# Attention and feed-forward kernel: the last two value bursts of a group go one slot forward, the maxima one slot back

## What is computed

```python
q = (seq2 + b_self) @ Wq + bq                     # 16 heads of 32
k = concat([seq1 + b_prev, seq2 + b_self]) @ Wk + bk
v = concat([seq1, seq2]) @ Wv + bv
score_prev = where(mask, q @ k[:l1].T * SCALE, -inf)   # 512 x 512 per head
score_self = (q * k[l1:]).sum(-1) * SCALE              # a row's own key
weights = softmax(concat([score_prev, score_self]))
attn = weights[..., :-1] @ v[:l1] + weights[..., -1:] * v[l1:]
x = x + attn @ Wo + bo
x = x + concat([gelu(x @ W1 + b1) @ W2 + b2, gelu(...) @ We[indices] + be])
```

## Time and profile before

| | |
|---|---|
| time, median of 3 runs | 1796.44 us (1793.42 to 1796.46) |
| profiled execution, its own time | 1807.21 us |
| its span | 1805.1 us |
| granted TensorE clock, mean | 0.976 |
| TensorE (PE) busy | 1719.9 us, 95% |
| VectorE (DVE) busy | 942.4 us, 52% |
| ScalarE (ACT) busy | 709.5 us, 39% |
| GpSimd (POOL) busy | 663.4 us, 37% |

### The profile page before, as it was taken

The page is one execution under the profiler, slowest core; times in us unless marked ns, Lnnn a source line. Parts: engine busy times, 40 slices in busy tenths (PEclk is TensorE's granted clock), DMA queues, the critical chain, the costliest instruction groups (busy, mean ns, idle before and its releaser), DMA issues.

```text
span 1805.1 us, 27962 instructions
## 1 busy us (share of the span) xinstructions
PE 1719.9 (95%) x8256; PEld 1262.1 (70%) x8256; DVE 942.4 (52%) x1430; ACT 709.5 (39%) x1259; POOL 663.4 (37%) x521
## 2 busy tenths in 40 slices
PE   6998999999999999999987899999999999999996
PEld 5765656666666666666652688888888888888885
DVE  4577576775866768757587643232232323232321
ACT  3253454444544445445344443323232323233222
POOL 3165577584874847748564301000010101010101
PEclk8999999999999999999996999999999999999998
DMA  6452444443534435244344342223131413232212
GB/s 143 76 114 51 91 103 107 86 97 73 120 90 91 96 85 119 69 103 87 80 110 121 109 122 50 68 48 86 46 87 41 87 52 75 61 66 72 47 30 53
DMA packets 370269, 149.45 MB, mean 83 GB/s; under 512 B 289226, under 2 KB 329162, under 8 KB 370194
## 3 DMA queue, kind: packets, MB, share of 16 engines
q1 hardware_dynamic: 364966, 146.28, 35.7%
q10 hardware_dynamic: 5228, 2.35, 0.5%
HBM read 70.41 MB, written 27.28 MB: 54 GB/s over the span
## 4 chain that ended last, share of the span: by engine, by line
PE 78%; issue 6%; DVE 5%; DMA 4%; SPq 3%; POOL 2%; ACT 1%; ACTq 0%; DVEq 0%; POOLq 0%
PE ps_proj L1258 14%; PE ps_max L1289 6%; PE ps_av L1210 6%; PE ps_av L1212 6%; PE ps_av L1211 6%; PE ps_av L1329 6%; PE ps_score L1316 5%; PE ps_proj L1210 3%; PE ps_proj L1211 3%; PE ps_proj L1212 3%; DMA stacks<-parts 3%; PE ps_score L1210 3%; PE ps_max L1212 3%; PE ps_score L1212 3%; PE ps_max L1210 3%
## 5 line engine op out<-in xcount | busy, mean ns | idle before, releaser
L729 ACT ACTIVATE p_f<-ps_score 128x512 f32<-128x512 f32 x512 | 303.8, 599 | 459.2 <-PE ps_score L1316 414.8
L941 DVE TENSOR_REDUCE m_col<-ps_max 128x1 f32<-128x512 f32 x512 | 328.7, 683 | 201.2 <-PE ps_max L1289 199.9
L604 POOL TENSOR_TENSOR p_sum<-p_sum,p_f 128x512 f32<-128x512 f32 x256 | 335.4, 1342 | 3.3 <-ACT p_f L729 3.3
L644 POOL TENSOR_TENSOR z_f<-z_f,a_raw 128x512 f32<-128x512 f32 x32 | 40.8, 1287 | 750.5 <-ACT z_f L842 730.0
L1135 DVE TENSOR_TENSOR h_lo<-h_f,h_hi 128x512 fp32r<-128x512 f32 x128 | 88.0, 687 | 412.2 <-ACT h_hi L833 412.1
L601 POOL TENSOR_TENSOR p_sum<-p_f 128x512 f32<-128x512 f32 x128 | 161.6, 1293 | 210.7 <-PE ps_av L1338 205.4
L1289 PE MATMUL ps_max<-stacks 97*128 97x512 f32 x512 | 189.3, 437 | 38.1 <-DVE m_col L941 19.4
L1258 PE MATMUL ps_proj<-in_hi,w_hi 128*128 128x512 f32 x512 | 207.8, 406 | 11.2 <-POOL in_lo L609 7.9
L1316 PE MATMUL ps_score<-stacks 99*128 99x512 f32 x512 | 209.0, 419 | 5.6 <-ACT p_f L729 5.4
L1210 PE MATMUL ps_av<-y_hi,w_hi 128*128 128x512 f32 x512 | 199.9, 390 | 6.6 <-ACT h_hi L833 3.8
L1258 PE MATMUL ps_proj<-in_lo,w_hi 128*128 128x512 f32 x512 | 205.6, 402 | 0.0
(11 more groups left out here) (122 smaller groups left out, 2729.1 us busy)
## 6 DMA issues: line engine op xcount, KB each, us to landing
stacks<-parts SPq DMA_DIRECT2D x384, 128.0 KB
raw<-in_x_dram SPq DMA_DIRECT2D x128, 64.0 KB, 2.3
raw<-in_fside_BxSxS_dram SPq DMA_DIRECT2D x128, 64.0 KB, 2.2
den<-own_scratch SPq DMA_DIRECT2D x128, 64.0 KB, 2.8
attn_scratch<-num SPq DMA_DIRECT2D x32, 256.0 KB, 3.0
x_raw<-in_x_dram SPq DMA_DIRECT2D x128, 64.0 KB, 2.2
we_raw<-in_L_cond_We_dram SPq DMA_DIRECT2D x32, 256.0 KB, 2.8
resid_scratch<-a_raw SPq DMA_DIRECT2D x32, 256.0 KB, 2.0
```

The lines of the kernel that those rows point to most:

```text
L604: pool.tensor_tensor(p_sum[:, j], p_sum[:, j], now, ALU.add).then_inc(sum_made, 1)
L729: act.activation(p_f[:, i % FLIGHT], ps_score[i % 2][:, :], ACT.Exp, scale=SCALE).then_inc(p_made, 1)
L941: dve.tensor_reduce(m_col[:, n % C, n // C:n // C + 1], ps_max[n % 2][:, :], AX.X, ALU.max).then_inc(max_made, 1)
```

## The change

`tiles_of_max` gives slot 0 no tile, and slots 1 to 8 two each; the bursts of `t` 2 and 3 of the group before follow the score (and the third, if there is one) of slot 0. The order of operations inside a slot is as before: score, maxima, values, thirds, bursts.

```diff
@@ -244,7 +244,7 @@
         def tiles_of_max(i):
 
-            ends = (2, 4, 6, 8, 10, 12, 14, TILES)
+            ends = (0, 2, 4, 6, 8, 10, 12, 14, TILES)
             return range(ends[i - 1] if i else 0, ends[i]) if i < len(ends) else range(0)
@@ -1392,7 +1392,7 @@
                         for n in thirds_of(g, i) if more else ():
                             project(*nxt2, order[n // 3], n % 3)
-                        if i == 1 and not (first and g == 0):
+                        if i == 0 and not (first and g == 0):
                             for t in (2, 3):
                                 value_burst(*after(b, g, -1), t)
```

## The result

The changed kernel takes **1802.30 us** (median of 20 runs, 1797.39 to 1810.76) against 1795.41 us for the one before (20 runs beside it, 1789.31 to 1801.08): a ratio of 1.004, 95% interval 1.0031 to 1.005. It is slower by 6.9 us, where the forecast was +2.5 us (1798.9) and "within 0.2%" the likeliest. Slower had a chance of 0.36, and 1802.30 lies in the range of 1789.5 to 1805.5.

What follows compares the result with a forecast made beforehand. TensorE, busy 95% of the span, was taken as the bound, leaving its idle stretches or clock. Terms: +4.9 over the batches, -2.9 for one long multiplication, +0.5 for another group, +2.5 us: 1798.9, range 1789.5 to 1805.5.

Steps and rivals of the forecast that it cites:

- The stack waits: First maxima pair of each group waits for the stack copy, 14.5 us in 27 places; all four per batch go.
- The bare gaps: Two maxima pairs with only a score between them: the second waits for VectorE, costing 0.58 to 1.02 us each.
- the sum of a steady batch: Groups 0 to 3 of batches 2 to 6: -1.68, +1.13, +0.46 and +0.96, together +0.87 us per batch.
- GpSimd's end plus one more pair: Group 2: slot 6's projection still starts when GpSimd finishes, and one more pair follows it, +0.46 us.
- The burst in slot 0: Eight matmuls moved from slot 1 wait little for the last exponential: no cost, at most 0.1 us per group.
- The sign of 30 us or more of waits for VectorE: In the changed trace the maxima's waits (L1289) for VectorE would rise from 19.4 us to 30 us or more.
- rival 2: Long multiplications decide: both lose their burst cost or one doesn't return, a further 7.4 us, down to 1790; chance 0.26.
- rival 1: Clock falls oftener in group 2, slot 6 waiting about 0.5 us longer for GpSimd: four more falls, 7.6 us, 1806.5; chance 0.22.
- my own sign: The forecast would be wrong if, among other things, TensorE's clock fell in places where it didn't before.
- the last batch's group 2: Counted as an ordinary group in the timed runs, +0.5 us.
- the long multiplication: VectorE's 8.98 us multiplication (L1016), twice in the trace: the burst hides in its wait, -2.9 us each; one assumed in timed runs.
- rival 3: No long multiplication in the timed runs at all: +4.9 + 1.0 = +5.9 us, 1802.3; chance 0.08.

Runs made afterwards that it cites:

- x4: Kernel before with only the bursts moved to slot 0, maxima left in slots 0 to 7: 1800.31 us, ratio 1.0009.
- x9: Kernel before with GpSimd making the last three low parts of the next batch's inputs ahead of additions: 1790.27 us, ratio 0.9968.
- x7: Changed kernel with GpSimd making the last three low parts of the next batch's inputs ahead of additions: 1793.77 us, ratio 0.9988.
- x11: x6 with GpSimd making the last three low parts of the next batch's inputs ahead of additions: 1768.21 us, ratio 0.9833.
- x6: x5 with a k2 projection third also moved from slot 9 to slot 7 in groups 1 and 3: 1795.40 us, ratio 0.9999.
- x1: Kernel before, unedited, run once more for a second trace: 1800.52 us.
- x5: Changed kernel with the first projection third moved from slot 0 to slot 1 in groups 1 and 3: 1786.33 us, ratio 0.9936.
- x2: Changed kernel, unedited, run once more for a second trace: 1808.78 us.
- x3: Changed kernel with the bursts back in slot 1, so only the maxima are later: 1806.54 us, ratio 1.0057.
- x8: Changed kernel with x6's thirds, x7's GpSimd order and group 2's thirds in slots 1, 2, 3, 5, 6, 7: 1832.80 us, ratio 1.0199.

## Why the prediction was right and where it was not

**The stack waits** go, all of them, as predicted (14.5 us to nothing).

**The bare gaps** are where the lists of thirds put them, and the sum of a steady batch holds: -1.6, +1.1, +0.45 and +0.86 us, +0.8 against +0.87 in the text; each group is within some 0.1 us of its term. That group 2's length is set by GpSimd's end plus one more pair (+0.46) is right: +0.45 in the one clean group of this trace. With every clock at 1.00 and group 0 of batch 0 at the -0.58 it was given, the lengths of the groups give +4.3 us where the sum has +4.9. The burst in slot 0 waits for nothing that counts. x4 and x9 confirm the prices away from the change. The sign of 30 us or more of waits for VectorE was set wrongly (16.4 us), as said above, and rival 2's 1790 is not what its terms give: 1796.44 - 0.9 - 7.4 is 1788.1.

**The clock** was held at nothing by the sum; rival 1 had it, at a chance of 0.22. The mechanism was named with its place and its bound: falls in 13 of 14 groups 2 instead of 7 of 14 in two traces of each kernel. The wait for GpSimd grew by 0.17 us only (0.45 against 0.28, both at full clock) and not by the 0.5 of the text. That the falls follow from it in large part is shown by x7 (two of seven) and by x11 against x6. What I brought against it, that a group 0 stays at 1.00, was one row: in the same trace group 0 of batch 0 falls to 0.89, and x1 has four. By my own sign I was wrong here, since the clock falls in groups where it had not. But the rival is right in only half of its account. Outside the groups 2, long multiplications apart, the two traces of before have six falls in batches 0 to 6 and the two of the changed kernel none, so that there are 13 falls on each side in all. As far as two traces each can tell, closing the hole of group 0 gave back about what that of group 2 cost, and neither the sum nor the rival had that.

**The steps that failed** are therefore two terms of the sum. The first is the last batch's group 2, which got a share of +0.5 us as an ordinary group: it is 29.57 us in x1 and 31.15 after, at a clock of 0.83 and 0.73, and 29.07 in x9 against 31.29 in x7, 1.6 and 2.2 us more. I have not taken it apart.

The second is the long multiplication, of which I subtracted 2.9 us and took one to be in the timed runs of both kernels, because the profiled execution stood 10.8 us above the median. The second trace of before has none and still lies 3.6 us above the median of its own set (1800.52 against 1796.88 us), with more falls. That the burst is hidden in such a hold is shown; that this saves 2.9 us is not, since x5 loses 8.7 us with its burst hidden, and x2 and x6 lose 5.8 and 5.5 in groups 0, which have other work to put into the hold. Without that deduction the sum is rival 3, 1802.3 us, which is the measured time; it had 0.08. That match is partly luck, as it has neither the falls in it nor what the last batch's group 2 grew by beyond an ordinary group.

**How much of the 6.9 us is the clock** can only be estimated. The mean granted clock is 0.9773 over the 20 runs of the changed kernel and 0.9783 over the 63 of the kernel before that stand beside x3 to x11: 0.001 of 1800 us is about 2 us, as much as the last batch's group 2 grew by. The comparison of x7 with x9 leaves 3.5 us without the wait for GpSimd, but these two are not free of falls either. So the larger part is stalls, and the clock some 2 us of it.

**What stays open** is why a fall happens in one batch and not in the next with the same hole (x5), and what lets GpSimd hold VectorE for one addition in most groups and for eight in a few. Neither was tried by itself, and no run repeats the last batch's group 2 with one thing changed.

## What to carry to other kernels

Price a shift in an interleaved order by its neighbours: write down what stands between each two users of a double buffer before and after, and take the price of an empty gap from a place in the trace that has one. Then look at what the saved time meets next: here it met a wait for GpSimd in a group with thin TensorE work, and earlier arrival became idle time in which the clock fell more often. Repairing that wait first, with work that was only queued in an unlucky order, made the gap-filling edits of x6 worth 27 us instead of nothing (x11). And take a second trace of the same kernel before you price something that happens twice in one: here it would have shown the long multiplications gone and the falls in other places.

## What the runs showed of the hardware

- A VectorE instruction with two inputs in SBUF can be held for the whole of an unbroken run of GpSimd instructions, not only for the one in flight: 8.98 us before, 9.04 in x2, 8.98 in x6, 10.69 in x5 for a multiplication that takes 1.5 us in most groups, and 12.40 in x8 for a subtraction that takes 0.69 elsewhere. Each ends some 0.55 us after GpSimd's run. The Trainium skill (SBUF — State Buffer, Who interferes with whom) has the one issued first hold the port for its own length; these rows go beyond it.
- TensorE's granted clock falls from 2.4 to 1.2 GHz for a while although TensorE never stops for long: in x3 no single wait before the falls of groups 2 is over 1.2 us, and it fell in seven groups of seven, with granted clocks such as 0.89 and 30.20 us for the group. In the changed kernel no wait there is over 0.6 us, and it fell in six of seven.
- Single runs of one kernel spread over 12 us (1789.31 to 1801.08), which is more than the effect of the change. In the 20 runs of the changed kernel the time goes with the mean granted clock: 1797.39 us at 0.980, 1810.76 us at 0.974.
